# Reordering one step of the key/value stage: accumulation ahead of the value projection, low V and cube later on VectorE

## The reference, cut to what matters

```python
q = (relu(q) + 1e-6) / scale;  k = (relu(k) + 1e-6) / scale
q_norm, k_norm = norm(q), norm(k)
q = q**3 / norm(q**3) * q_norm
k = k**3 / norm(k**3) * k_norm
z = 1 / (q . sum_over_tokens(k) + 1e-6)
kv_state = einsum('bjc,bjd->bcd', k, v)          # per head
out = einsum('bic,bcd->bid', q, kv_state) * z + depthwise_5x5(v)
x = x + out @ Wproj.T + bproj
```

## Time and profile before

| | us |
|---|---|
| median of three runs | 3926.62 |
| lowest and highest | 3916.32, 3932.86 |
| the profiled execution | 3932.86 |
| its span in the profile | 3930.8 |
| TensorE busy | 3542.5 (90%) |
| VectorE busy | 2972.1 (76%) |
| ScalarE busy | 2711.0 (69%) |
| GpSimd busy | 1426.4 (36%) |

### The profile page before, as it was taken

One profiled execution on the slowest core, in us unless ns is written; L12 is line 12 of the kernel. 1 busy time (PEld: TensorE's weight loads), 2 busy tenths in 40 slices (PEclk: granted clock), 3 DMA queues, 4 the chain that ended last, 5 costly groups with the idle time before them and its releaser, 6 DMA issues.

```text
span 3930.8 us, 96093 instructions
## 1 busy us (share of the span) xinstructions
PE 3542.5 (90%) x27980; PEld 2861.4 (73%) x27980; DVE 2972.1 (76%) x8235; ACT 2711.0 (69%) x7348; POOL 1426.4 (36%) x1318
## 2 busy tenths in 40 slices
PE   0569999999999999989999998999999899999797
PEld 0238777777877778777777877777787777778686
DVE  6767887868778786877868788786878878585756
ACT  2247776776777667676766767777677767677675
POOL 4632442514334252443514244351424425140302
PEclk9889999999999999999999999999999999999999
DMA  4672534536354462635436263443636354260302
GB/s 156 205 238 66 169 105 138 169 90 189 110 154 120 129 177 79 189 107 150 134 110 192 73 186 117 141 141 112 179 92 181 102 148 127 83 181 21 103 17 76
DMA packets 560048, 516.44 MB, mean 131 GB/s; under 512 B 97600, under 2 KB 491968, under 8 KB 559552
## 3 DMA queue, kind: packets, MB, share of 16 engines
q1 hardware_dynamic: 555200, 508.99, 43.9%
q10 hardware_dynamic: 4352, 1.57, 0.2%
HBM read 351.06 MB, written 134.22 MB: 123 GB/s over the span
## 4 chain that ended last, share of the span: by engine, by line
PE 42%; DVE 26%; issue 14%; ACT 13%; DMA 2%; DVEq 2%; SPq 1%; ACTq 0%; POOL 0%; POOLq 0%
PE F L1518 9%; PE VAB L1518 7%; PE F L1557 6%; ACT K L1295 6%; PE T L1529 5%; PE VAB L1557 5%; DVE F L975 4%; DVE XR L1064 3%; DVE XR L1057 3%; DVE XHL L969 3%; DVE XR L1046 2%; ACT K L1301 2%; PE PP L1608 2%; DVE ST L962 1%; DVE RATIO L989 1%
## 5 line engine op out<-in xcount | busy, mean ns | idle before, releaser
L1518 PE MATMUL F<-WQ,XHL 128*128 128x256 f16 x6144 | 822.7, 275 | 27.3 <-ACT V L1335 19.0
L650 POOL TENSOR_TENSOR XR<-XR,V 128x512 f32<-128x512 f32 x256 | 326.0, 1274 | 1038.9 <-DVE XR L1046 1038.9
L1518 PEld LDWEIGHTS F<-WQ,XHL 128*128 128x128 f16 (+1 forms) x6144 | 603.4, 99 | 105.6 <-issue 33.6
L1295 ACT ACTIVATE K<-F,SCAL 128x256 f32<-128x256 f32 x1024 | 476.3, 471 | 292.3 <-DVE F L975 279.7
L1504 PE MATMUL SM<-SL,BD 128*128 128x512 f16 x2688 | 634.9, 385 | 0.0
L634 POOL TENSOR_TENSOR SL<-PL,SL 128x1122 f16<-128x1122 f32 x112 | 260.1, 2322 | 1031.8 <-DVE SL L947 1031.8
L1301 ACT ACTIVATE K<-K,SCAL 128x256 f32<-128x256 f32 x1024 | 514.0, 510 | 160.9 <-DVE K L981 160.8
L981 DVE TENSOR_TENSOR K<-K,F 128x512 f32<-128x512 f32 x512 | 351.6, 687 | 282.0 <-ACT K L1295 184.0
L975 DVE TENSOR_TENSOR F<-F,FL 128x512 f32<-128x512 f32 x512 | 353.9, 691 | 154.4 <-PE F L1520 148.3
L1504 PEld LDWEIGHTS SM<-SL,BD 128*128 128x128 f16 x2688 | 261.0, 97 | 284.1
L1608 PE MATMUL PP<-XR,WP 128*128 128x256 f16 x3072 | 388.9, 278 | 67.8 <-DVE XR L1064 67.8
(11 more groups left out here) (194 smaller groups left out, 6954.6 us busy)
## 6 DMA issues: line engine op xcount, KB each, us to landing
XR<-xr SPq DMA_DIRECT2D x132, 512.0 KB, 5.3
U<-x SPq DMA_DIRECT2D x256, 256.0 KB, 3.8
XR<-x SPq DMA_DIRECT2D x256, 256.0 KB, 4.1
out<-XR SPq DMA_DIRECT2D x256, 256.0 KB, 3.8
PL<-xp SPq DMA_DIRECT2D x112, 561.0 KB, 3.8
RX<-xr SPq DMA_DIRECT2D x118, 512.0 KB, 4.0
x<-RX SPq DMA_DIRECT2D x448, 128.0 KB, 2.1
BD<-RX SPq DMA_DIRECT2D x240, 96.0 KB, 2.2
```

The source lines that it names most:

```text
L650: g_.tensor_tensor(o, o, fm, ALU.add).then_inc(o_rdy, 2)
L1295: a.activation(K2[:, p, ts], F[p][:, ts], ACT.Square, scale=inv_a, accum_out=S2[:, 2 * p + t:2 * p + t + 1]).then_inc(f_sq, 1)
L1518: t_.matmul(o, XHL[:, xa, h, at], WQ[:, wa, h, c0:c0 + C], start=(k == 0), stop=False)
```

## The change

On TensorE, `accumulate_state` of the half two steps back is issued between `keys` and `values`. On VectorE, `ratio` of the half before is issued ahead of `low_v`, and `scale_k` of the half before ahead of `cube`. The instructions, their operands and their waits stay the same; the order before the loop, after it, on ScalarE and on GpSimd isn't touched.

```diff
@@ -1009,10 +1009,10 @@
             def step_kv(b, u, p):
                 n = b * 2 * PAIRS + 2 * u + p
                 floor_max(n, p)
+                ratio(n - 1, 1 - p, S2, S6)
                 low_v(b, u - 1 + p, 1 - p)
-                ratio(n - 1, 1 - p, S2, S6)
+                scale_k(n - 1, 1 - p)
                 cube(n, p)
-                scale_k(n - 1, 1 - p)
 
@@ -1542,8 +1542,8 @@
 
             def step_kv(b, u, p):
                 keys(b, u, p)
+                accumulate_state(b, u - 1, p)
                 values(b, u, p)
-                accumulate_state(b, u - 1, p)
```

## The result

The changed kernel takes 3970.05 us (median of four runs, 3966.69 to 3974.39) against 3929.47 us for the kernel before (four runs, 3916.32 to 3932.86). Over all timings on record, 21 of the changed kernel (3964.66 to 3980.88), the ratio is 1.0115, with a 95% interval of 1.010 to 1.013. The direction and the place were as forecast, and so were the signs: waits for the scaling of K beside GpSimd, none in the steps of the last two images, and one short and one long wait at each end. The loss is 40.6 us between the two medians of four, and some 45 us by the ratio, where I had 29.

What follows compares the result with a forecast made beforehand. TensorE was taken to be full inside the stage, at 3.95 us a step. The terms, 14 x 1.8 us for the loop plus 4 for the stage ends, gave 29 us on 3926.62: 3955, range 3934 to 3974.

Steps and rivals of the forecast that it cites:

- the signs: Changed profile: steps some 4.2 us beside GpSimd, 3.95 otherwise; at stage ends a short wait, then one over 2.5 us.
- No gain inside the stage: TensorE never waits inside the stage, 3.95 us a step, so nothing can be gained there.
- The carried loop: VectorE's new order puts scaling and low V into the step-to-step loop: 3.67 us, a margin of 0.28 against 3.95.
- What eats the margin: Scalings of K beside GpSimd take 0.57 us more for about 8 steps an image: 4.24 us a step.
- My aside on a lock: VectorE and GpSimd lock a shared port pair; a steady unlucky alignment would give up to 9 us an image.
- What TensorE feels: Of VectorE's 2.3 us lag, all beyond 0.48 us becomes TensorE's delay: 1.8 us in each of 14 images.
- The idea of a reserve: Scaled K is ready 0.76 us before TensorE wants it, so that much lag is covered.
- The end of the stage: Copy of V starts later, so the last accumulation comes 0.27 us later in 16 images: 4 us.
- The clock: Rivals on granted clock after stage-end waits: worse, about 3985 us, 6%; better, 3907 us if the loop costs nothing, 7%.
- The low stretches: After the waits at a stage's end the granted clock is at half: 1.7 us in 14 of 16 images.
- My rival for the worse: One long idle time at the stage's end doubles the half-clock time: 31 us more, about 3985; 6%.
- The price that I gave the low stretch behind a stage: Half clock after a stage's end costs 1.7 us in 14 images, 24 us back if avoided.

Runs made afterwards that it cites:

- e2: VectorE's new order alone on the kernel before, TensorE in its old order: ratio 1.0061.
- e3: The whole change, with VectorE's hardware loop over the first four units written out: ratio 1.0115 to the kernel before.
- e4: The whole change, but low V stays ahead of ratio on VectorE: ratio 1.0107 to the kernel before.
- e1: TensorE's edit alone on the kernel before (accumulation between keys and values), VectorE in its old order: ratio 1.0116.
- e7: The whole change, with GpSimd's 17 large instructions on 24 of 32 columns from image 2 on: ratio 1.0078 to the kernel before.
- e11: The whole change, with GpSimd's 17 large instructions on 28 of 32 columns from image 2 on: ratio 1.0045 to the kernel before.
- e12: The whole change, with GpSimd's 17 large instructions on 20 of 32 columns from image 2 on: ratio 1.006 to the kernel before.
- e6: The kernel before, with GpSimd's 17 large instructions on 1 of 32 columns from image 2 on: ratio 1.0002.
- e9: The kernel before, with TensorE's accumulation between the two tiles of the values and VectorE in its old order: ratio 1.0047.
- e8: Kernel before; last step of a stage only: TensorE accumulates ahead of values, ScalarE does sixth powers, V's state copy, root, then V's high part: 0.9933, 3896.31 us.

## Why the prediction was right in its direction and low in its size

**No gain inside the stage.** Right: TensorE was full, and its steps without GpSimd are 3.95 us before and after.

**The carried loop.** Its existence is shown by e2, and my sum for its free length is near: 1.13 + 0.46 + 0.78 + 0.52 + 0.71 = 3.60 us outside the hardware loop in the changed kernel, against my 3.67; inside it the step from ratio to low V is 0.60 to 0.69 us where I took 0.50. But e3 and e4, which shorten the loop by 0.15 to 0.8 us, gain next to nothing (0 and 0.08%, within the noise), and e1 loses it all without the loop. So the loop doesn't decide, though I had put it so.

**The step that failed** is "What eats the margin": the excess of a pair of scalings as an average, 0.57 us, added to the loop to give 4.24 us a step. The measured step is 4.47, and it isn't a sum: terms taken out of the loop in e3 and e4 didn't shorten it. My aside on a lock there had a steady alignment in it, but only as an extreme, and the sum went by the average. A scaling that is under way late has to wait for GpSimd's instruction to end, everything behind it is dated from that end, and the next one again finds GpSimd in the middle of an instruction. A step beside GpSimd lasts a whole number of its instructions: three, 3 x 1.49 = 4.47 us. With 2.7 us an image in place of 1.8, the 14 images cost 38.0 us instead of 25. The widths show it (e7, e11, e12), and e1, with another order on VectorE, still takes six instructions for two steps.

**What TensorE feels** is the second step that failed. The idea of a reserve was right, but it weighs more than I gave it: e1 takes away only the reserve and loses everything, while e2 keeps it and loses 0.6%, by a lag that builds up. The scaled K is ready 1.4 us before TensorE wants it in the kernel before, and a pair waits for GpSimd for up to 1.26 us (1.87 less 0.61): covered, so nothing is lost, and e6 gains nothing. TensorE's edit takes 1.52 us of this reserve and gives 0.57 back, since the cube no longer waits: 0.45 is left (e1; 0.4 in its last two images, by the starts). I had counted a TensorE delay only as what is left of VectorE's lag. But a delayed TensorE delays its own next keys, and by them floor, squares, cube and scaling, so the loop closes over TensorE without VectorE's new order; that way is read from the waits in the code, and that it needs no new order on VectorE is shown by e1. e9, with 1.2 us of reserve, has 3.2 us of loss in the steps instead of 38: far from in proportion, and near what a threshold at the longest wait would give. No run lies between 0.45 and 1.2 us.

**The end of the stage.** The term was 0.27 us and measured 0.39: the copy of V starts at phase 4.25 (1991.20 to 1986.95), 0.30 us after the values' last matmul and not 0.20. 6.2 us instead of 4.

**The clock.** Not the cause of the loss. The low stretches moved: 4.5 us more behind the stages, 11.8 less at their openings in the profiled runs. My rival for the worse did come in kind, since after one wait of 2.47 us all 16 images have the low stretch, but at 4.5 us and not 31. I had also misread the number of images that have it before: 13, not 14. The openings stood in no term of mine. There is luck in how near 3955 came: the stages lost 44.2 us where I had 29, and the openings gave 11.8 back. The price that I gave the low stretch behind a stage, 24 us in all, is an upper value: e8, which removes it, is 17.6 us shorter there in its profiled execution, and by the medians 11 us are left for the clock and all else. Why the stretch appears in some images and not in others after equal waits stays open.

## What to carry to other kernels

Before moving an instruction on a saturated engine, work out for each of its inputs how long before the demand it is ready, and compare this reserve with the longest wait that its producer can meet, not with the average; one that is just covered today is worth more than its idle time suggests. Two engines that keep each other waiting for whole instructions can fall into step, and then the time of a step is a whole number of the other's instructions. Here taking up to 0.8 us out of the loop gained nothing, and GpSimd instructions that were shorter by an eighth gained more than ones shorter by a quarter. Where no other engine's instructions are in the way, as at the end of this stage, the same reordering of TensorE, together with ScalarE's new order, paid (e8).

## What the runs showed of the hardware that I had not expected

A pair of VectorE's scalings (128x256 in fp32, two instructions, 0.61 us alone) ends 0.40 us after the end of the GpSimd instruction that it met, in step after step of the changed kernel. In e1 every second pair has GpSimd's next instruction start between its two scalings (1949.82 to 1951.22), and ends 0.15 us after that one, at 1951.37. With GpSimd's instructions on 20, 24, 28 and 32 columns the kernel lost 0.60, 0.78, 0.45 and 1.15%. In the hardware loop, low V starts 0.59 to 0.70 us after the ratio does, and 0.45 outside it, also in the images in which GpSimd rests; with the loop written out (e3) it is 0.45 everywhere. Two waits of 0.72 and 1.00 us at the end of a stage left the clock at full in all 16 images, where 1.47 and 1.26 us were followed by about 3 us at half in 13 before and in 9 of e6, and one of 2.47 us behind a short one in all 16 of the changed kernel.
